# A two-block recurrence and feed-forward kernel on one core: residuals by transposes, expert masks on GpSimd, the last slot in channel chunks, and a new order on every engine

## The chip, the cores and the metric

The kernel runs on one core of a Trainium2 chip. The time is device microseconds (us) from start to end of one execution, the median of several runs. The five engines are TensorE (PE, with its weight loads as PEld), VectorE (DVE), ScalarE (ACT), GpSimd (POOL) and SyncE (SP), which here only issues transfers. Each runs its own list of instructions in the order in which the program wrote them, and waits on semaphores for the others.

## The reference

Four batches ("slots" b = 0 to 3) of x, 256 positions by 256 channels, go through two blocks. The core of it, shortened:

```python
x = x + moe(bi_wkv(x, side, side, w0, u0, cond), A, Bw, Wg)
x = x + ffn(bi_wkv(x, side, side, w1, u1, cond), w1, b1, w2, b2)

def bi_wkv(r, k, v, w, u, t):       # per channel, along the 256 positions
    ek = exp(min(k, 30)); ekv = ek * v
    nf, df = forward scans of a = a * decay + (ekv or ek)
    nb, db = the same scans backward
    euk = exp(min(u + k, 30))
    return sigmoid(r) * (nf + nb - ekv + euk * v) / max(df + db - ek + euk, 1e-8) * (0.8 + 0.2 * tf)

def moe(x, A, Bw, Wg):              # 8 experts of rank 64, the best one per position
    prob = softmax(x @ Wg.T); chosen = argmax(prob)
    return (((x @ A.T) * onehot(chosen)) @ Bw) * 4 * prob[chosen]

def ffn(x, w1, b1, w2, b2):         # 1024 hidden units, weights made -1, 0 or 1
    return gelu(x @ q(w1).T + b1) @ q(w2).T + b2
    # q(w) = sign(w) where |w| >= 0.7 * mean(|w|), else 0
```

## The kernel before, in words

Everything is transposed on chip: channels lie on the 128 partitions (two chunks, c = 0 and 1) and positions along the free dimension. A layer's slot passes through these helpers, whose names and lines the prediction uses:

- `forward` and `backward` (scans, lines 794 and 828, two instructions of 128x256 each) for the numerator (NUM) and the denominator (DEN), on DVE. Between the two `seed` (line 286) rescales the last column. `own_keys` (778, DVE), `own_values` (242), `add_num` (248) and `times_sigmoid` / `times_tanh` (254, 265) are the rest of the numerator, mostly on POOL; `add_den` (835) is the rest of the denominator.
- The reciprocal is `log_den` and `reciprocal` on ACT (529, 534), one Newton step on DVE (`den_times_rec` 840, then `ratio` 857, or `refine_rec` 846 and `product` 863), and `num_times_rec` (405) on POOL.
- The expert block: `gate_logits` (1141), `gate`, `gate_index` and `expert_mask` (870 to 892) on DVE, `transpose_mask`, `expert_in` (1156, fp32, in two halves k), `select_expert` (900, DVE), and `expert_out` (1172, fp32), which accumulates on the residual that `place_residual` (1130) put into its bank. `keep_x1` (599) copies the sum out.
- The feed-forward block: `xin_high` and `xin_low` (306 or 305, and 292) split the input into two fp32r parts; `hidden(b, j)` (1224) multiplies both parts with a quarter of w1, 8 matmuls; `gelus` (611, ACT); `h_high` and `h_low` (305 or 306, and 298) split h; `ffn_out(b, j, n)` (1258) multiplies with a quarter of w2 for half n of the positions, 4 matmuls, onto what `place_output` (1250) put there.
- `keep_warm(n)` and `warm_up(n)` (1041, 1035) are transposes whose results are not used.

Each engine's order is a flat list of such calls at the end of its block (POOL from line 418, ACT from 614, DVE from 909, PE from 1266); nothing else sets the order. A helper that takes an engine as its first argument can be put on DVE, POOL or ACT. The two placings multiply fp32 data with the fp32 identity:

```python
pe.matmul(bank[Y_BANK][:, c * T + n * P:c * T + (n + 1) * P],
          x_nat[:, NT * b + n, c * P:(c + 1) * P], ident[:, :], start=(c == 0 and n == 0), stop=False)
```

The expert mask compares a row of expert numbers with the chosen expert's number and multiplies by its probability. On DVE its three inputs lie in PSUM, which POOL cannot be given here:

```python
dve.tensor_scalar(mask[:, i % (2 * NT)], expert_ps, bank[DVE_BANK][:, IDX_AT + i:IDX_AT + i + 1],
                  bank[DVE_BANK][:, GREC_AT + i:GREC_AT + i + 1], ALU.is_equal, ALU.mult).then_inc(mask_ready, 1)
```

Results leave through two staging buffers: `result` (slots 0 to 2) and `last_result` (two halves of slot 3).

Of the kernel before, what the change touches and what calls it, by code (L numbers as in the profile page):

```python
# [6 lines left out]
ALU = mybir.AluOpType  # L7
# [17 lines left out]
def adaln_ffn_kernel(nc, x, fside, cond, w_l0, u_l0, A, Bw, Wg, w_l1, u_l1, w1, b1, w2, b2, out):  # L25
# [23 lines left out]
    with ExitStack() as ctx:  # L49
# [51 lines left out]
        gsum = sb("gsum", [P, NI])  # L101
        mask = sb("mask", [P, 2 * NT, P])
# [75 lines left out]
        g_bank = [7, 4] * 4 + [6, 7, 4] * 2 + [6, 7]  # L178
# [3 lines left out]

        NEG_AT, IDX_AT, GREC_AT, EXPERT_AT = 4 * ND, 4 * ND + 2, 4 * ND + 2 + NI, P
# [5 lines left out]
        expert_ps = bank[DVE_BANK][:, EXPERT_AT:EXPERT_AT + P]  # L189
# [112 lines left out]

        def copy_on(eng, dst, src):
# [77 lines left out]
        def _(pool):  # L381
# [24 lines left out]

            def factors():
# [15 lines left out]
            seed(pool, 0, 0, DEN)  # L423
            seed(pool, 0, 1, DEN)
            seed(pool, 0, 0, NUM)
            times_values(pool, 1)
            own_values(pool, 0, 0)
            clip_keys(pool, 2)
            add_num(pool, 0, 0)
            times_sigmoid(pool, 0)  # L430
            own_values(pool, 0, 1)
            seed(pool, 0, 1, NUM)
            num_times_rec(0, 0)
            add_num(pool, 0, 1)
            seed(pool, 0, 2, DEN)
            times_values(pool, 2)
            times_sigmoid(pool, 1)
            num_times_rec(0, 1)
            clip_keys(pool, 3)
            own_values(pool, 0, 3)  # L440
            own_values(pool, 0, 2)
            seed(pool, 0, 3, DEN)
            times_values(pool, 3)
            seed(pool, 0, 2, NUM)
            add_num(pool, 0, 2)
            times_sigmoid(pool, 2)
            num_times_rec(0, 2)
            seed(pool, 0, 3, NUM)
            own_values(pool, 1, 0)
            add_one(0)  # L450
            seed(pool, 1, 0, NUM)
            add_num(pool, 0, 3)
            times_sigmoid(pool, 3)
            seed(pool, 1, 0, DEN)
            num_times_rec(0, 3)
            add_num(pool, 1, 0)
            times_tanh(pool, 0)
            add_b2(0)
            num_times_rec(1, 0)
# [3 lines left out]
            add_one(1)  # L463
            xin_low(pool, 0)
            own_values(pool, 1, 2)
            seed(pool, 1, 1, NUM)
            own_values(pool, 1, 3)
# [3 lines left out]
            seed(pool, 1, 2, DEN)  # L471
            add_b2(2)
            xin_low(pool, 1)
            h_low(pool, 0, 1)
            seed(pool, 1, 2, NUM)
            add_one(2)
            h_low(pool, 0, 2)
            add_num(pool, 1, 2)
            h_low(pool, 1, 0)
            h_low(pool, 1, 2)  # L480
            h_low(pool, 1, 3)
            add_one(3)
            h_low(pool, 2, 0)
            add_b2(3)
            h_low(pool, 3, 1)
            h_low(pool, 3, 3)

        @block.scalar
        def _(act):
# [115 lines left out]

            def gelus(b, j):
# [791 lines left out]
```

## Time and profile before

| | us |
|---|---|
| median of 3 runs (103.58 to 103.70) | 103.62 |
| the profiled execution's own time | 102.58 |
| its span, first to last instruction or transfer | 100.8 |
| PE busy in the span | 93.5 |
| DVE busy | 86.7 |
| ACT busy | 80.2 |
| POOL busy | 66.1 |

The profiled execution is 1.8 us longer than its span (start and end of the program) and 1.0 us under the median. "Busy" is the union of an engine's records. Matmul records overlap, since matmuls are pipelined: what one costs is the distance between starts. Transfers fill the first 20 us (inputs, 5.26 MB) and then only the outputs remain.

### The profile page before, as it was taken

What the parts mean: (1) busy time and instruction counts of PE and PEld (TensorE: products, weight loads), DVE (VectorE), ACT (ScalarE), POOL (GpSimd) and SP (SyncE); (2) the same over time, 40 slices, a digit from 0 to 9 for tenths busy, and PEclk for the clock granted to TensorE, in tenths of its full rate; (3) what the DMA queues carried; (4) which work ended last, traced back from release to release, by engine and by line L of the source; (5) the groups of instructions that cost most, each with busy time, mean ns of one, the idle gap of its engine ahead of it and who ended that gap; (6) DMA issues with size and microseconds to landing.
All of it is one profiled execution on the core that took longest, in us unless ns stands there. A gap on an engine that the chain in (4) does not pass through costs nothing. (4 is left out here: it accounts for less than half of the span.)

```text
span 100.8 us, 2134 instructions
## 1 busy us (share of the span) xinstructions
PE 93.5 (93%) x665; PEld 85.0 (84%) x665; DVE 86.7 (86%) x203; ACT 80.2 (80%) x144; POOL 66.1 (66%) x90
## 2 busy tenths in 40 slices
PE   3999779989988999999999999999999999999980
PEld 2688659978878889888888888989999999999970
DVE  3389999999999999999999999999997997883330
ACT  4369999999986679999667499998986899986520
POOL 4058679979984796069868987999980867005310
DMA  1899999700000000000000000000000020200005
GB/s 33 243 292 336 298 228 385 281 3 0 3 0 0 3 0 7 0 0 0 0 3 7 0 0 0 0 0 0 0 7 0 0 104 33 72 7 3 0 0 208
DMA packets 6886, 6.43 MB, mean 64 GB/s; under 512 B 2370, under 2 KB 6492, under 8 KB 6876
## 3 DMA queue, kind: packets, MB, share of 16 engines
q1 hardware_dynamic: 6868, 6.31, 20.2%
q8 instruction: 5, 0.08, 0.3%
q14 instruction: 5, 0.04, 0.1%
q10 hardware_dynamic: 8, 0.00, 0.0%
HBM read 5.26 MB, written 1.05 MB: 63 GB/s over the span
## 5 line engine op out<-in xcount | busy, mean ns | idle before, releaser
L298 POOL TENSOR_TENSOR h_lo<-h,h_hi 128x512 fp32r<-128x512 f32 x9 | 12.3, 1367 | 12.5 <-DVE h_hi L306 7.1
L794 DVE TENSOR_TENSOR_SCAN run<-bank,kv 128x256 f32<-128x256 f32 x32 | 20.1, 674 | 0.2
L1156 PE MATMUL bank<-num,AT 128*128 128x256 f32 x64 | 15.5, 384 | 0.7 <-DVE hm L900 0.5
L1258 PE MATMUL bank<-w2T,h_hi 128*128 128x256 f32 x64 | 15.9, 286 | 0.0
L611 ACT ACTIVATE h<-bank,bT 128x256 f32<-128x256 f32 x32 | 13.1, 478 | 3.2 <-PE bank L1224 2.9
L1224 PE MATMUL bank<-xin_hi,w1T 128*128 128x256 f32 x64 | 15.5, 283 | 0.0
L1258 PE MATMUL bank<-w2T,h_lo 128*128 128x256 f32 x64 | 15.6, 281 | 0.0
L1224 PE MATMUL bank<-xin_lo,w1T 128*128 128x256 f32 x64 | 15.2, 277 | 0.0
L1172 PE MATMUL bank<-hm,BT 128*128 128x256 f32 x64 | 14.6, 381 | 0.0
L1156 PEld LDWEIGHTS bank<-num,AT 128*128 128x128 f32 x64 | 11.6, 190 | 2.2 <-issue 0.9
L1172 PEld LDWEIGHTS bank<-hm,BT 128*128 128x128 f32 x64 | 11.9, 190 | 1.5
L1224 PEld LDWEIGHTS bank<-xin_hi,w1T 128*128 128x128 f32 x64 | 12.0, 188 | 0.6 <-POOL xin_lo L292 0.4
L248 POOL TENSOR_TENSOR num<-num,own 128x512 f32<-128x512 f32 x7 | 8.9, 1278 | 5.2 <-DVE num L828 5.1
L1258 PEld LDWEIGHTS bank<-w2T,h_lo 128*128 128x128 f32 x64 | 12.0, 188 | 0.0
L1258 PEld LDWEIGHTS bank<-w2T,h_hi 128*128 128x128 f32 x64 | 12.0, 188 | 0.0
L1224 PEld LDWEIGHTS bank<-xin_lo,w1T 128*128 128x128 f32 x64 | 12.0, 188 | 0.0
L242 POOL TENSOR_TENSOR own<-own,vs 128x512 f32<-128x512 f32 x8 | 10.2, 1275 | 1.4 <-DVE own L778 1.3
L828 DVE TENSOR_TENSOR_SCAN bank<-bank,run 128x256 f32<-128x256 f32 x16 | 10.2, 681 | 0.0
L828 DVE TENSOR_TENSOR_SCAN num<-bank,run 128x256 f32<-128x256 f32 x16 | 10.1, 671 | 0.0
L405 POOL TENSOR_TENSOR num<-num,run 128x512 f32<-128x512 f32 x5 | 6.4, 1279 | 1.2 <-DVE run L794 0.9
L529 ACT ACTIVATE run<-bank 128x512 f32<-128x512 f32 x8 | 4.8, 605 | 2.9 <-DVE bank L835 2.9
L305 ACT ACTIVATE h_hi<-h 128x512 fp32r<-128x512 f32 x11 | 6.8, 635 | 0.3 <-ACT h L611 0.2
(141 smaller groups left out, 226.1 us busy)
## 6 DMA issues: line engine op xcount, KB each, us to landing
w_nat<-in_L_ffn_w_dram SPq DMA_DIRECT2D x2, 1024.0 KB, 8.5
F_nat<-in_fside_BxSxS_dram SPq DMA_DIRECT2D x4, 256.0 KB, 3.1
x_nat<-in_x_dram SPq DMA_DIRECT2D x4, 256.0 KB, 4.9
out_dram<-outb SPq DMA_DIRECT2D x3, 256.0 KB, 2.1
A_nat<-in_L_ffn_A_dram SPq DMA_DIRECT2D x1, 512.0 KB, 5.6
B_nat<-in_L_ffn_Bw_dram SPq DMA_DIRECT2D x2, 256.0 KB, 6.3
out_dram<-outb SPq DMA_DIRECT2D x2, 128.0 KB, 1.9
wv_rows<-in_L_cond_w_dram SPq DMA_DIRECT2D x2, 1.0 KB
```

Of the source, the lines that this page charges most:

```text
L242: eng.tensor_tensor(own[:, r, :, NUM, :], own[:, r, :, DEN, :], vs[:, b], ALU.mult).then_inc(ownv_ready[r], 1)
L248: eng.tensor_tensor(num_at(l, b), num_at(l, b), own[:, r, :, NUM, :], ALU.add).then_inc(num_ready[r], 1)
L298: eng.tensor_tensor(h_lo[:, b % 2, 2 * j:2 * j + 2], h32[:, b % 2, 2 * j:2 * j + 2], h_hi[:, b % 2, 2 * j:2 * j + 2].bitcast(F32), ALU.sub ...
L305: return eng.activation(dst, src, ACT.Copy)
L405: pool.tensor_tensor(num_at(l, b), num_at(l, b), run[:, r, :, DEN, :], ALU.mult).then_inc(q_ready[r], 1)
L611: act.activation(h32[:, b % 2, f], bank[g_bank[NJ * b + j]][:, (f % 2) * T:(f % 2 + 1) * T], ACT.Gelu, bias=bT[:, f:f + 1], scale=0.5).the ...
L794: dve.tensor_tensor_scan(run[:, r, c, q], decay_ps[:, l, c, b:b + 1].broadcast_to([P, T]), kv[:, b, c, q], 0.0, ALU.mult, ALU.add).then_in ...
L828: dve.tensor_tensor_scan(into[:, c, ::-1], decay_ps[:, l, c, b:b + 1].broadcast_to([P, T]), run[:, r, c, q, ::-1], 0.0, ALU.mult, ALU.add) ...
L1156: mm = pe.matmul(bank[H_BANK + k][:, (m % 2) * T:(m % 2 + 1) * T], AT[:, c, m * P:(m + 1) * P], num_at(0, b)[:, c], start=(c == 0), stop=( ...
L1172: mm = pe.matmul(bank[Y_BANK][:, o * T:(o + 1) * T], BT[:, m, o * P:(o + 1) * P], hm[:, b % 2, m], start=False, stop=(o == NC - 1 and m == ...
L1224: mm = pe.matmul(bank[g_bank[g]][:, (f % 2) * T:(f % 2 + 1) * T], w1T[:, c, f * P:(f + 1) * P], part[:, b % 2, c], start=(c == 0 and part ...
L1258: mm = pe.matmul(o_region(b, n), part[:, b % 2, f, n * P:(n + 1) * P], w2T[:, f], start=False, stop=(f == NF - 1 and part is h_lo and (n = ...
```

## The change

1. `place_residual` and `place_output` pass `is_transpose=True`, on the same data and the same identity.
2. `expert_mask` moves to POOL. The chosen number and the reciprocal of the softmax sum go into small SBUF tiles (`chosen`, `prob`) in place of PSUM columns; DVE keeps the reciprocal as `gate_reciprocal`, and no longer copies the row of expert numbers to PSUM.
3. Slot 3 of layer 1: the denominator's steps, the product and the split into xin parts run per channel chunk (`last_...` helpers), each chunk's denominator in a PSUM bank of its own (2 and 3); `last_hidden(j, c)` issues the four matmuls of one chunk. The last quarter of h is split and multiplied per tile f (`last_gelu`, `last_h_high`, `last_h_low`, `last_ffn_out`). `hidden(3, 3)` uses bank 2 in place of 7.
4. The first `expert_in` half no longer waits for the transposed Bw.
5. All four engines' lists are reordered, and some calls change engine: `clip_keys(1)`, `times_tanh(2)`, `times_tanh(3)`, `add_num(1, 3)`, `h_low(0, 3)`, `h_low(2, 2)` and `seed(1, 3, DEN)` go from DVE to POOL; `own_values(1, 3)`, `h_low(1, 0)`, `h_low(1, 2)`, `h_low(3, 1)`, `h_low(3, 3)` and four `seed` calls from POOL to DVE; `xin_high(2)`, `h_high(2, 1)`, `h_high(3, 3)` and `result(0)` to `result(2)` from ACT to DVE; `xin_high(1)`, `h_high(2, 2)`, `h_high(3, 1)` and `last_result(0)` from DVE to ACT.

The diff, cut to its core:

```diff
-                                  x_nat[:, NT * b + n, c * P:(c + 1) * P], ident[:, :], start=(c == 0 and n == 0), stop=False)
+                                  x_nat[:, NT * b + n, c * P:(c + 1) * P], ident[:, :], start=(c == 0 and n == 0), stop=False, is_transpose=True)
...
-                                  start=(c == 0 and (n == 0 or b == NB - 1)), stop=False)
+                                  start=(c == 0 and (n == 0 or b == NB - 1)), stop=False, is_transpose=True)
...
+            def expert_mask(b):
+                pool.wait_ge(consts_ready, 4 + NE)
+                pool.wait_ge(index_steps, (NT + 1) * (b + 1))
+                pool.wait_ge(grec_ready, b + 1)
+                if b >= 2:
+                    pool.wait_ge(mask_psum, b - 1)
+                for i in range(NT * b, NT * (b + 1)):
+                    pool.tensor_scalar(mask[:, i % (2 * NT)], expert_of[:, :], chosen[:, i:i + 1], prob[:, i:i + 1],
+                                       ALU.is_equal, ALU.mult).then_inc(mask_ready, 1)
...
-                dve.tensor_copy(bank[DVE_BANK][:, IDX_AT + NT * b:IDX_AT + NT * (b + 1)], idx8[:, both, 0]).then_inc(index_steps, 1)
+                dve.tensor_copy(chosen[:, both], idx8[:, both, 0]).then_inc(index_steps, 1)
...
+                dve.reciprocal(prob[:, both], gsum[:, both]).then_inc(grec_ready, 1)
...
-        g_bank = [7, 4] * 4 + [6, 7, 4] * 2 + [6, 7]
+        g_bank = [7, 4] * 4 + [6, 7, 4] * 2 + [6, 2]
...
+            def last_den_times_rec(c):
+                dve.wait_ge(rec_ready[LR], LU + c + 1)
+                den = last_den(c)
+                dve.tensor_tensor(den, den, run[:, LR, c, DEN, :], ALU.mult).then_inc(dr_ready[LR], 1)
...
+            def last_hidden(j, c):
+                g = NJ * LB + j
+                pe.wait_ge(xlo_ready[LB % 2], LB // 2 + 1 + c)
+                if c == 0:
+                    hidden_bank_free(g)
+                for f in (2 * j, 2 * j + 1):
+                    for part in (xin_hi, xin_lo):
+                        mm = pe.matmul(bank[g_bank[g]][:, (f % 2) * T:(f % 2 + 1) * T], w1T[:, c, f * P:(f + 1) * P],
+                                       part[:, LB % 2, c], start=(c == 0 and f == 2 * j and part is xin_hi),
+                                       stop=(c == NC - 1 and f == 2 * j + 1 and part is xin_lo))
+                if c == NC - 1:
+                    mm.then_inc(g_psum, 1)
```

The start of the new DVE list, from `decays()` to the first `gate`:

```python
forward_chunk(0, 0, DEN, 0); forward_chunk(0, 0, DEN, 1); inverse_gains(); seed(dve, 0, 0, DEN)
backward(0, 0, DEN); forward(0, 0, NUM); place_factors(); forward(0, 1, DEN); own_keys(0, 0)
backward(0, 0, NUM); add_den(0, 0); forward(0, 1, NUM); forward(0, 2, DEN); own_keys(0, 1)
den_times_rec(0, 0); own_keys(0, 2); ratio(0, 0); backward(0, 1, NUM); seed(dve, 0, 2, DEN); gate(0)
```

Its part from `gate(3)` to the end of slot 3's input:

```python
gate(3); add_den(1, 1); gate_index(3); gate_reciprocal(3); forward(1, 2, NUM); own_keys(1, 2)
backward(1, 1, NUM); forward(1, 2, DEN); select_expert(3, 0); den_times_rec(1, 1); select_expert(3, 1)
refine_rec(1, 1); seed(dve, 1, 2, NUM); seed(dve, 1, 2, DEN); product(1, 1); backward(1, 2, DEN)
add_den(1, 2); backward(1, 2, NUM); forward(1, 3, NUM); den_times_rec(1, 2); forward(1, 3, DEN)
refine_rec(1, 2); seed(dve, 1, 3, NUM); own_keys(1, 3); product(1, 2); xin_high(dve, 2); h_low(dve, 1, 0)
xin_low(dve, 2); own_values(dve, 1, 3); backward(1, 3, NUM); backward_last_chunk(0)
backward_last_chunk(1); add_last_den(0); add_last_den(1); h_low(dve, 1, 2); h_high(dve, 2, 0)
h_low(dve, 1, 1); result(dve, 0); last_den_times_rec(0); refine_last_rec(0); last_product(0)
last_xin_high(0); last_den_times_rec(1); last_xin_low(0); refine_last_rec(1); h_high(dve, 2, 1)
last_product(1); last_xin_high(1); last_xin_low(1)
```

On PE `warm_up(4)` before the x transposes becomes `warm_up(8)`, `keep_warm(19)` and `(27)` become `(19)`, `(15)` and, behind the first `expert_in` half, `(8)`. `transpose_B(1)` comes behind `gate_logits(0)`, and `expert_out(0)` before the first `transpose_weights`. From slot 3's hidden layer on, the PE list is:

```python
last_hidden(0, 0); ffn_out(1, 3, 0); ffn_out(1, 3, 1); last_hidden(1, 0); last_hidden(0, 1)
last_hidden(2, 0); last_hidden(1, 1); last_hidden(3, 0); place_output(3); last_hidden(2, 1)
ffn_out(3, 0, n); ffn_out(2, 1, n); ffn_out(3, 1, n); last_hidden(3, 1); ffn_out(3, 2, n)
ffn_out(2, 2, n); last_ffn_out(6, n); ffn_out(2, 3, n); last_ffn_out(7, n)      # each for n = 0, 1
```

## Rows read from the trace of the kernel before

**Rows 1.** The page's first part: busy time, share of the span, instructions.

```profile
PE 93.5 (93%) x665; PEld 85.0 (84%) x665; DVE 86.7 (86%) x203; ACT 80.2 (80%) x144; POOL 66.1 (66%) x90
```

**Rows 2.** The chain that ended last, in order: start, us, engine, line.

```profile
61.46 0.89 PE bank L1130 x8
62.35 1.83 PE bank L1224 x16
...
65.20 3.46 PE bank L1172 x16
...
93.07 4.75 PE bank L1258 x40
...
97.84 0.42 DVE outb L306
```

**Rows 3.** Timeline of DVE, 46 to 51 us: start, duration, line, operation.

```profile
46.66 1.26 DVE L828 TENSOR_TENSOR_SCAN num<-bank,run 128x256 f32<-128x256 f32 x2
47.83 1.25 DVE L828 TENSOR_TENSOR_SCAN bank<-bank,run 128x256 f32<-128x256 f32 x2
49.00 0.67 DVE L857 SCALAR_TENSOR_TENSOR num<-bank,num 128x512 f32<-128x512 f32 x1
49.59 0.68 DVE L900 TENSOR_TENSOR hm<-bank,mask_rows 128x512 f32<-128x512 f32 x1
```

**Rows 4.** Stretches: us, then busy PE, PEld, DVE, ACT, POOL, PE clock, DMA.

```profile
15.00:20.00 5.00, 5.00 (x46) 4.91 (x46) 5.00 (x9) 5.00 (x10) 4.92 (x5) 1.00 0.93 344
...
70.00:75.00 5.00, 4.95 (x43) 4.78 (x42) 5.00 (x11) 4.97 (x11) 4.33 (x6) 1.00 0.01 3
```

**Rows 5.** Timeline of PE, 12 to 28 us.

```profile
12.69 0.66 PE L1110 MATMUL bank<-ident,A_nat 128*128 128x128 f32 x4 [0.69 <-DMA A_nat<-in_L_ffn_A_dram]
13.28 0.29 PE L1098 MATMUL bank<-ident,Wg_nat 8*128 8x8 f32 x2
...
18.02 3.11 PE L1041 MATMUL bank<-ident 128*128 128x128 f32 x27
21.39 1.06 PE L1141 MATMUL bank<-WgT,num 128*128 128x8 f32 x8 [0.26 <-DVE num L857]
...
24.88 1.05 PE L1130 MATMUL bank<-ident,x_nat 128*128 128x128 f32 x8
25.77 1.89 PE L1156 MATMUL bank<-num,AT 128*128 128x256 f32 x8
```

**Rows 6.** Timeline of DVE: mask, expert selection and slot 3's last input part.

```profile
25.79 0.16 DVE L886 RECIPROCAL bank<-gsum 128x2 f32<-128x2 f32 x1
...
26.73 0.68 DVE L857 SCALAR_TENSOR_TENSOR num<-bank,num 128x512 f32<-128x512 f32 x1
...
62.65 1.28 DVE L900 TENSOR_TENSOR hm<-bank,mask_rows 128x512 f32<-128x512 f32 x2
63.84 0.69 DVE L846 SCALAR_TENSOR_TENSOR bank<-bank,run 128x512 f32<-128x512 f32 x1
...
86.37 0.69 DVE L292 TENSOR_TENSOR xin_lo<-sig,xin_hi 128x512 fp32r<-128x512 f32 x1
```

**Rows 7.** Groups by line with shapes: busy us, mean ns of one.

```profile
L227 POOL TENSOR_SCALAR kv<-ek_raw 128x512 f32<-128x512 f32 x2 | 1.2, 612 | 0.7 <-ACT ek_raw L509 0.6
...
L231 POOL TENSOR_SCALAR kv<-ek_raw 128x256 f32<-128x256 f32 x2 | 0.8, 400 | 3.2 <-ACT ek_raw L513 3.2
```

**Rows 8.** Timeline of DVE: a small instruction and one with two SBUF inputs.

```profile
23.45 0.17 DVE L907 TENSOR_SCALAR thr<-thr 128x2 f32<-128x2 f32 x1
...
73.91 0.67 DVE L265 TENSOR_TENSOR num<-num,sig 128x512 f32<-128x512 f32 x1
```

**Rows 9.** Timeline of POOL at the same two times.

```profile
22.29 1.27 POOL L236 TENSOR_TENSOR kv<-kv,vs 128x512 f32<-128x512 f32 x1
...
74.09 1.63 POOL L298 TENSOR_TENSOR h_lo<-h,h_hi 128x512 fp32r<-128x512 f32 x1 [0.43 <-ACT h_hi L305]
```

**Rows 10.** The last transfers, as SP issues them.

```profile
97.94 0.96 SPq L376 DMA_DIRECT2D out_dram<-outb  x2
```

More of the change, by code:

```diff
@@ L101, in adaln_ffn_kernel @@
         gsum = sb("gsum", [P, NI])
+        chosen = sb("chosen", [P, NI])
+        prob = sb("prob", [P, NI])
         mask = sb("mask", [P, 2 * NT, P])
@@ L718, in _ @@
             gelus(3, 1)
+            h_high(act, 3, 1)
             gelus(3, 2)
             h_high(act, 3, 2)
-            gelus(3, 3)
-            h_high(act, 3, 3)
-            result(act, 2)
+            last_gelu(6)
+            last_gelu(7)
+            last_result(act, 0)
         @block.vector
@@ L956, in _ @@
             select_expert(1, 0)
+            own_keys(0, 3)
+            gate(2)
+            forward(0, 3, NUM)
+            backward(0, 3, DEN)
+            gate_index(2)
+            gate_reciprocal(2)
             add_den(0, 3)
-            forward(1, 0, NUM)
-            gate(2)
+            backward(1, 0, DEN)
             backward(0, 3, NUM)
-            gate_index(2)
-            forward(1, 0, DEN)
+            add_den(1, 0)
+            own_keys(1, 1)
+            select_expert(2, 1)
+            select_expert(2, 0)
@@ L963, in _ @@
+            forward(1, 1, DEN)
+            den_times_rec(1, 0)
             den_times_rec(0, 3)
-            expert_mask(2)
-            backward(1, 0, NUM)
-            backward(1, 0, DEN)
+            ratio(1, 0)
             ratio(0, 3)
-            select_expert(2, 0)
-            add_den(1, 0)
-            select_expert(2, 1)
-            forward(1, 1, DEN)
+            forward(1, 1, NUM)
+            backward(1, 1, DEN)
             gate(3)
-            den_times_rec(1, 0)
+            add_den(1, 1)
@@ L974, in _ @@
             gate_index(3)
-            ratio(1, 0)
-            own_keys(1, 1)
-            backward(1, 1, DEN)
-            own_keys(1, 3)
-            add_den(1, 1)
+            gate_reciprocal(3)
+            forward(1, 2, NUM)
             own_keys(1, 2)
-            forward(1, 1, NUM)
-            expert_mask(3)
             backward(1, 1, NUM)
+            forward(1, 2, DEN)
+            select_expert(3, 0)
             den_times_rec(1, 1)
-            select_expert(3, 0)
             select_expert(3, 1)
@@ L998, in _ @@
-            times_tanh(dve, 2)
+            refine_rec(1, 2)
             seed(dve, 1, 3, NUM)
-            seed(dve, 1, 3, DEN)
-            refine_rec(1, 2)
+            own_keys(1, 3)
             product(1, 2)
-            h_low(dve, 0, 3)
-            h_low(dve, 1, 1)
-            xin_low(dve, 2)
-            backward(1, 3, DEN)
-            backward(1, 3, NUM)
-            add_den(1, 3)
-            add_num(dve, 1, 3)
-            h_high(dve, 2, 0)
-            times_tanh(dve, 3)
-            den_times_rec(1, 3)
@@ L1013, in _ @@
-            refine_rec(1, 3)
-            product(1, 3)
-            xin_high(dve, 3)
-            xin_low(dve, 3)
+            xin_high(dve, 2)
+            h_low(dve, 1, 0)
+            xin_low(dve, 2)
+            own_values(dve, 1, 3)
+            backward(1, 3, NUM)
+            backward_last_chunk(0)
+            backward_last_chunk(1)
+            add_last_den(0)
+            add_last_den(1)
+            h_low(dve, 1, 2)
+            h_high(dve, 2, 0)
+            h_low(dve, 1, 1)
+            result(dve, 0)
@@ L1329, in _ @@
             hidden(1, 1)
+            place_output(1)
             ffn_out(0, 1, 0)
```

445 lines of the change are left out of this document (257 added, 188 removed).

## The prediction

> **What bounds the kernel now.** I read four views. The page's first part [rows 1] shows PE busy 93% and DVE 86%; neither figure is a verdict, because matmul records overlap. The chain of waits [rows 2] says where the end comes from: from 61.46 us on it runs through PE alone, and from expert_out(3) at 65.20 to the last copy at 97.84 PE never waits. Further back it goes over to DVE, and DVE's timeline [rows 3] shows why: its instructions start one behind the other with no pause. From these starts come my DVE units: a pair of scans 1.17 us (46.66 to 47.83 to 49.00), a 128x512 instruction 0.59 (49.00 to 49.59). So there are two full engines: DVE decides when PE gets its inputs, up to about 64 us, and PE's own work decides the rest. The stretches [rows 4] show the same (all four compute engines full in 15 to 20 us and nearly so in 70 to 75), and a granted PE clock of 1.00 (2.4 GHz) in both.
>
> **The placings.** A placing is 4 fp32 matmuls in 8 records. From its start to the next group's is 0.89 us (24.88 to 25.77) [rows 5]. The same instruction as a transpose is one record: four cost 0.59 us (12.69 to 13.28), and in a long row 27 take from 18.02 to about 21.1, 0.115 each, so four would cost 0.46. The floor is that 0.46 and the ceiling 0.89, no gain at all. I take 0.50, between the two rows for real transposes, so 0.39 saved per placing and 3.1 us over eight, on the engine that is never idle at the end. The rows show no transpose that opens an accumulation; if the mode change itself costs something it is inside the ceiling.
>
> **The first slot.** gate_logits(0) starts at 21.39 [rows 5], released by DVE's ratio(0, 0). The new DVE list puts behind that ratio a backward pair for the denominator (1.17), one for the numerator (1.17) and an add_den (0.59), and clip_keys(1) leaves for POOL (0.34). Before it come own_keys(0, 2), two instructions of 128x256 (0.8), and a seed (0.1). That is -3.27 + 0.9 = -2.4, so gate_logits(0) can start at 19.0. The POOL work behind it also has to fit: own_values, add_num, times_sigmoid and num_times_rec are four instructions of the 1.27 us kind [rows 9], behind own_keys(0, 0) at about 12.1, so 17.4 at best, with DVE needing it at 18.4: hidden by one microsecond. If POOL slips by more, ratio(0, 0) slips with it.
>
> **The masks.** On DVE two masks and their reciprocal take 25.79 to 26.73 [rows 6], 0.94 us, of which about 0.15 (the reciprocal) stays: 0.79 saved per slot, 3.1 over four. On POOL no such instruction is to be seen. One input at 128x256 costs 0.40 and at 128x512 0.61 [rows 7]; by their slope a 128x128 one is 0.3. The ends are 0.2 (a quarter of 0.61 and no fixed cost) and the 1.27 of a two-input 128x512. I take 0.3, because the shape lies next to the 0.40. Two per slot make 0.6, and POOL has room (66% busy [rows 1]). The mask waits for the gate's index and reciprocal, with num_times_rec, times_tanh or seed queued behind it on POOL; by my walk POOL reaches it about when the gate is done or earlier by under 1 us, and what stands behind it waits for a later DVE scan anyway.
>
> **Up to expert_out(3).** Two sums must meet. PE: from gate_logits(0) to expert_out(3) took 65.20 - 21.39 = 43.8 us. Five placings fall in it (-1.95), and keep_warm(8) (+0.9) and transpose_B(1) (+0.56) come into it, so 43.3, and 19.0 + 43.3 = 62.3. DVE: select_expert(3, 1) was over at 63.84 [rows 6]. Removed in front of it are the masks (3.1), the clip (0.34) and own_keys(1, 3) (0.79); added are both forward pairs of slot (1, 2) instead of none (2.34) and seeds (0.15). That gives 63.84 - 1.74 = 62.1. Both sums say that expert_out(3) starts at 62.3, 2.9 us earlier. That is the front of the gain: ratio(0, 0) earlier for PE, masks off DVE, and neither engine alone would give it. It assumes that the gaps in PE's list, which I count at about 3 us from gate_logits(0) on, stay as they are.
>
> **After expert_out(3).** Here the work is the same but for three placings, 1.2 us less. So PE would be done at 97.84 - 2.9 - 1.2 = 93.7, 4.1 us earlier. The cover to check is slot 3. Its last input part ended at 86.37 + 0.69 = 87.06 [rows 6], 0.2 us ahead of PE. In the new list DVE loses before that point masks 3.1, clip 0.34, two times_tanh and an add_num 1.8, h_low(0, 3) 0.6, xin_high(1) 0.35 and some 1.3 of its own waits, 7.5 in all, and gains own_values 0.6, two h_low 1.2, xin_high(2) and h_high(2, 1) 0.7, result(0) 0.6, seeds 0.3 and 0.5 for splitting five instructions into chunks: 3.9. So the second chunk is there at 83.4 and the first some 1.5 earlier, 81.9, while PE reaches last_hidden(0, 0) at about 82.2. In ACT the new list puts slot 3's logarithm, exponential and two table loads before gelus(2, 1), which by the same count ends at 81.3. Three engines thus arrive within a microsecond of each other. With no slack on any, I put 0.5 us down for the join; the chunks are what keeps it so small, since PE may start with the first half.
>
> **The end.** The last copy and its transfer are as before: SP issues two stores from 97.94 [rows 10]. result(2) now runs on DVE some 0.5 us before the last copy on the same engine, and may push it by 0.1, which I leave inside the 0.5.
>
> **Sum.** -2.9 - 1.2 + 0.5 = -3.6 us on the profiled execution, whose time is 102.58 (span 100.8 and 1.8 around it): 99.0. The median of the runs is 1.04 above that execution, so I forecast 103.62 - 3.6 = 100.0.
>
> **Rivals.**
> - *Only the placings pay.* The order is so tight that any slip on POOL or ACT (their work has no measured counterpart in the new order) opens a gap on PE, and the earlier start is waited away. Then the 5 placings from 61.46 on are left, 2.0 us: 101.6. For it speaks that DVE, PE and ACT are all full in 70 to 75 us [rows 4]; against it that two independent sums give the same start.
> - *The order closes gaps too.* Of the 3 us of PE's gaps up to 61 us, one goes as well and the join is free: 103.62 - 5.1 = 98.5.
> - *The transposes save nothing.* Placings stay at 0.89; 3.1 of the gain goes, and 0.5 is left: 103.1. Rows for transposes of loaded data [rows 5] speak against it.
> - *VectorE and GpSimd get in each other's way*, the case in which it becomes slower. POOL's h_low at 74.09 took 1.63 us instead of 1.27, while DVE's times_tanh at 73.91 also read two SBUF tensors [rows 8, 9]: 0.36 lost. The change puts such instructions on DVE while POOL is at work (own_values(1, 3), h_low(1, 0), h_low(1, 2), xin_low(2), xin_high(2), h_high(2, 0), h_high(2, 1)), and makes the four copies into `chosen` and the four reciprocals into `prob` SBUF to SBUF. If each of these 15 waited on DVE for half a POOL instruction, 0.64, DVE would be 9.6 us later in all, of which the sums above cover 4.1 and about 0.5 of slack: 5.0 late, 108.6. It turns slower once the mean wait of the 15 passes 0.3. Against it: the 128x2 instruction at 23.45 is SBUF to SBUF, fell into POOL's 22.29 to 23.56, and took 0.17 with no delay [rows 8, 9]. The Trainium skill (SBUF — State Buffer, Who interferes with whom) says that VectorE and GpSimd share a port pair, locked for a whole instruction by whichever starts first, when VectorE copies within SBUF in a two-port mode or has two SBUF inputs. By that rule the small copies would stall, and the time would be the one of this rival; the trace's small row speaks against it for the small ones, and the 1.63 speaks for it for the large ones.
>
> **Chances.** Forecast 0.48, more than that (98.5) 0.12, only the placings 0.22, transposes save nothing 0.06, port conflict 0.09 and some other wait with no gain 0.03. A measurement here can tell about 0.2% from no change. Faster: 0.48 + 0.12 + 0.22 + 0.05 = 0.87; within 0.2% 0.04; slower 0.09. The range for 8 in 10 takes in the better case partly and the placings alone: 98.7 to 102.4 us, leaving out the two last cases and the ends of the others.
>
> **What would show it.** Placings: L1130 and L1250 with half the records, 0.5 us to the next group. First slot: gate_logits(0) near 19.0. Masks: POOL instructions of 128x128 near 0.3, and DVE free of them. expert_out(3) near 62.3, PE then without pauses, slot 3's first matmuls near 82.5, last copy near 94.2. The forecast is wrong if DVE shows instructions well over their old durations (port conflict), if PE waits for POOL's xin_low or h_low, or if slot 3's reciprocal on ACT comes late.

## The result and the profile after

The changed kernel takes **105.06 us** (median of 4 runs, 104.09 to 105.27) where the kernel before, in the same session, takes 103.60 (4 runs, 103.51 to 103.70). The ratio is 1.0142 with a 95% interval of 1.0086 to 1.0197: slower by 1.4%, where 100.0 us and a range of 98.7 to 102.4 had been forecast. The executions of either kernel differ in the granted TensorE clock, and like must be compared with like. The kernel before ran 43 times beside the experiments below; nine of these were slow ones (more than 1.5% above the fastest) and are left out. Of the other 34, 20 held a mean clock of 0.995 or more (median 102.57 us) and 14 had 0.983 or less (median 103.57). The changed kernel took 104.09 in its one execution at 1.00 and 105.0, 105.13 and 105.27 at 0.983 to 0.984. The change costs 1.5 to 1.6 us at either clock.

The rows below are of the profiled execution of the changed kernel (105.0 us, span 103.2, clock 0.983). First its page, busy time as in [rows 1] and the group of the new masks:

```profile
PE 90.8 (88%) x633; PEld 81.3 (79%) x633; DVE 91.2 (88%) x206; ACT 79.0 (77%) x144; POOL 72.2 (70%) x96
L423 POOL TENSOR_SCALAR mask<-expert_of,chosen,prob 128x128 f32<-128x128 f32 x8 | 6.3, 797 | 2.3 <-DVE prob L974 2.3
```

DVE gave up the masks and is nevertheless busy for 91.2 us instead of 86.7. The last part of the chain of waits, beside [rows 2] (start, us, engine, line):

```profile
86.79 1.28 issue
88.06 0.42 DVE sig L911
...
88.51 0.30 DVE xin_hi L916
...
88.84 0.44 DVE xin_lo L921
...
89.32 2.11 PE bank L1330 x16
91.42 0.44 PE bank L1357 x4
...
98.09 0.96 PE bank L1365 x8
```

Before, the chain ran in PE from 61.46 us on. Now it comes to PE only at 89.32 us; ahead of that it goes through DVE's last input part of slot 3. What stands there as "issue" for 1.28 us is DVE inside one instruction. DVE's timeline shows it (start, duration, line, operation):

```profile
22.61 0.88 DVE L968 CAST chosen<-idx 128x2 f32<-128x2 uint32 x1
...
73.55 1.33 DVE L314 CAST xin_hi<-sig 128x512 fp32r<-128x512 f32 x1
...
75.40 1.09 DVE L292 TENSOR_TENSOR xin_lo<-sig,xin_hi 128x512 fp32r<-128x512 f32 x1
...
80.01 1.70 DVE L298 TENSOR_TENSOR h_lo<-h,h_hi 128x512 fp32r<-128x512 f32 x1
81.63 0.41 DVE L314 CAST h_hi<-h 128x512 fp32r<-128x512 f32 x1
81.97 0.68 DVE L298 TENSOR_TENSOR h_lo<-h,h_hi 128x512 fp32r<-128x512 f32 x1
...
84.54 0.65 DVE L916 CAST xin_hi<-sig 128x256 fp32r<-128x256 f32 x1
...
85.45 0.93 DVE L921 TENSOR_TENSOR xin_lo<-sig,xin_hi 128x256 fp32r<-128x256 f32 x1
...
86.63 1.51 DVE L314 CAST h_hi<-h 128x512 fp32r<-128x512 f32 x1
```

The same form has two durations: h_lo takes 1.70 and then 0.68, the h_hi cast 0.41 and then 1.51. POOL's timeline at these times tells which is which:

```profile
22.18 1.28 POOL L254 TENSOR_TENSOR num<-num,sig 128x512 f32<-128x512 f32 x1
...
79.87 1.29 POOL L265 TENSOR_TENSOR num<-num,sig 128x512 f32<-128x512 f32 x1
...
84.99 1.10 POOL L274 TENSOR_TENSOR x_nat<-x_nat,bT 128x512 f32<-128x512 f32 x1
86.56 1.29 POOL L298 TENSOR_TENSOR h_lo<-h,h_hi 128x512 fp32r<-128x512 f32 x1 [0.47 <-ACT h_hi L313]
```

POOL's times_tanh starts at 79.87 and ends at 81.16; DVE's h_lo, begun at 80.01, ends at 81.71, 0.55 behind it, which is about its own length. POOL's h_lo ends at 87.85, DVE's cast at 88.14, 0.29 behind it. Each of the long DVE instructions is an ordinary one that first waits out the POOL instruction that was already under way. There are seven, and together they lose 0.71 + 0.90 + 0.40 + 1.01 + 0.36 + 0.51 + 1.10 = 5.0 us. The reciprocals into `prob`, which are also SBUF to SBUF, do not wait: this one lies well inside POOL's instruction and takes its usual 0.15.

```profile
33.00 0.15 DVE L974 RECIPROCAL prob<-gsum 128x2 f32<-128x2 f32 x1
...
32.55 1.28 POOL L254 TENSOR_TENSOR num<-num,sig 128x512 f32<-128x512 f32 x1
```

On PE the waits show so:

```profile
76.55 0.39 PE L1317 MATMUL bank<-xin_hi,w1T 128*128 128x256 f32 x1 [1.51 <-DVE xin_lo L292]
...
86.43 0.39 PE L1330 MATMUL bank<-xin_hi,w1T 128*128 128x256 f32 x1 [0.20 <-DVE xin_lo L921]
...
89.32 0.39 PE L1330 MATMUL bank<-xin_hi,w1T 128*128 128x256 f32 x1 [0.77 <-DVE xin_lo L921]
```

### The profile page after: what moved, and what is told of

The parts are those of the page before. It is cut to its first block, busy times and chain, and to the rows that moved or that the text cites. A ratio compares the mean times of both kernels' runs of the same rounds, so it can differ in the third digit from the quotient of the medians.

```text
span 103.2 us, 2087 instructions
## 1 busy us (share of the span) xinstructions
PE 90.8 (88%) x633; PEld 81.3 (79%) x633; DVE 91.2 (88%) x206; ACT 79.0 (77%) x144; POOL 72.2 (70%) x96
## 4 chain that ended last, share of the span: by engine, by line
PE 38%; DVE 25%; ACT 18%; issue 14%; DVEq 1%; POOL 1%; POOLq 0%
PE bank L1267 9%; PE bank L1365 6%; PE bank L1251 5%; DVE bank L862 4%; PE bank L1129 4%; PE bank L1330 3%; DVE run L828 3%; PE bank L1160 3%; DVE num L862 2%; DVE h_lo L298 2%; ACT sig L567 2%; PE bank L1235 2%; DVE bank L874 2%; PE bank L1135 2%; PE bank L1291 1%
## 5 line engine op out<-in xcount | busy, mean ns | idle before, releaser
L1267 PE MATMUL bank<-hm,BT 128*128 128x256 f32 x64 | 16.3, 412 | 0.2 <-issue 0.2
L248 POOL TENSOR_TENSOR num<-num,own 128x512 f32<-128x512 f32 x8 | 10.3, 1286 | 4.7 <-DVE num L862 4.4
L1317 PE MATMUL bank<-xin_hi,w1T 128*128 128x256 f32 x48 | 11.9, 287 | 1.5 <-DVE xin_lo L292 1.5
L1317 PE MATMUL bank<-xin_lo,w1T 128*128 128x256 f32 x48 | 11.5, 279 | 0.0
L1317 PEld LDWEIGHTS bank<-xin_hi,w1T 128*128 128x128 f32 x48 | 9.0, 188 | 1.9 <-DVE xin_lo L292 1.7
L298 POOL TENSOR_TENSOR h_lo<-h,h_hi 128x512 fp32r<-128x512 f32 x7 | 9.3, 1346 | 1.5 <-DVE h_hi L314 1.0
L1317 PEld LDWEIGHTS bank<-xin_lo,w1T 128*128 128x128 f32 x48 | 9.1, 189 | 0.0
L423 POOL TENSOR_SCALAR mask<-expert_of,chosen,prob 128x128 f32<-128x128 f32 x8 | 6.3, 797 | 2.3 <-DVE prob L974 2.3
L298 DVE TENSOR_TENSOR h_lo<-h,h_hi 128x512 fp32r<-128x512 f32 x8 | 6.5, 813 | 1.2 <-ACT h_hi L313 1.1
L812 DVE SCALAR_TENSOR_TENSOR own<-ek_raw,bank 128x256 f32<-128x256 f32 x16 | 6.9, 470 | 0.0
```

The costliest lines, as they stand in the source:

```text
L248: eng.tensor_tensor(num_at(l, b), num_at(l, b), own[:, r, :, NUM, :], ALU.add).then_inc(num_ready[r], 1)
L298: eng.tensor_tensor(h_lo[:, b % 2, 2 * j:2 * j + 2], h32[:, b % 2, 2 * j:2 * j + 2], h_hi[:, b % 2, 2 * j:2 * j + 2].bitcast(F32), ALU.sub ...
L423: pool.tensor_scalar(mask[:, i % (2 * NT)], expert_of[:, :], chosen[:, i:i + 1], prob[:, i:i + 1], ALU.is_equal, ALU.mult).then_inc(mask_r ...
L812: dve.scalar_tensor_tensor(own[:, r, c, DEN], ek_raw[:, b, c], scale_ps[:, l, c, b:b + 1], cap_ps[:, l, c, b:b + 1].broadcast_to([P, T]), ...
L1267: mm = pe.matmul(bank[Y_BANK][:, o * T:(o + 1) * T], BT[:, m, o * P:(o + 1) * P], hm[:, b % 2, m], start=False, stop=(o == NC - 1 and m == ...
L1317: mm = pe.matmul(bank[g_bank[g]][:, (f % 2) * T:(f % 2 + 1) * T], w1T[:, c, f * P:(f + 1) * P], part[:, b % 2, c], start=(c == 0 and part ...
```

## The experiments

All times are medians; the kernel before, measured anew beside each set of runs, took 103.47 to 103.55 us.

**1. The placings alone.** The kernel before, with nothing but the two placings made transposes:

```diff
-    ident[:, :], start=(c == 0 and n == 0), stop=False)
+    ident[:, :], start=(c == 0 and n == 0), stop=False, is_transpose=True)
...
-    start=(c == 0 and (n == 0 or b == NB - 1)), stop=False)
+    start=(c == 0 and (n == 0 or b == NB - 1)), stop=False, is_transpose=True)
```

> The kernel before with one edit: both placings as transposes, nothing else of the change. Theory A (VectorE's slot 3 holds the end): in the kernel before, slot 3's last input part was ready at 87.06 us and TensorE reached it at 87.24, and seven of the eight placings lie ahead of that point, so TensorE would only wait for VectorE instead. Only 0.2 us come back at once, and at most the 1.3 us that VectorE waited for ScalarE at 77.8 and 83.7: 0.3 to 1.5 us faster than before, 102.1 to 103.3. Theory B (the prediction's: TensorE's own work from 61 us on is the end, so each placing pays): 2.0 to 3.1 us faster, 100.5 to 101.6. Both expect half the records and 0.35 to 0.5 us from a placing to the next group.

It took 102.76 us (10 runs), ratio 0.9928 (0.9873 to 0.9983): a gain of 0.8 us (0.2 to 1.3) from an edit that takes 8 x 0.45 = 3.6 us of work from PE. PE's timeline of this kernel, with the last placing and the matmuls behind it:

```profile
86.65 0.60 PE L1250 MATMUL bank<-ident,x_nat 128*128 128x128 f32 x4
87.77 0.38 PE L1224 MATMUL bank<-xin_hi,w1T 128*128 128x256 f32 x1 [0.52 <-DVE xin_lo L292]
```

PE waits for slot 3's input, which ends at 87.02 + 0.69 = 87.71 on DVE. Already in the kernel before, that input had only 0.2 us in hand. So PE's work by itself was not what the end could be shortened by: the interval leaves out the 2.0 us and more that it would have given.

The same trace shows, on DVE and POOL, the instruction on which the prediction's argument against the port conflict rests:

```profile
23.40 1.21 DVE L907 TENSOR_SCALAR thr<-thr 128x2 f32<-128x2 f32 x1
...
23.31 1.28 POOL L254 TENSOR_TENSOR num<-num,sig 128x512 f32<-128x512 f32 x1
```

In the kernel before it took 0.17 [rows 8]. Here POOL began 0.09 us ahead of it, and it ends at 24.61, 0.02 behind POOL: 1.04 us of waiting for two columns. Everything behind it on DVE is later by about as much (select_expert(3, 0) starts at 63.62 instead of 62.65), so this one execution, of 103.12 us, does not tell how long PE would have waited without it. Of the executions of this kernel at a clock of 0.995 or more, four took 101.87 to 102.19 us and three 103.07 to 103.41; whether this wait is what parts them is not shown, since only one was profiled.

**2. The changed kernel with the placings as matmuls.**

```diff
-    ident[:, :], start=(c == 0 and n == 0), stop=False, is_transpose=True)
+    ident[:, :], start=(c == 0 and n == 0), stop=False)
...
-    start=(c == 0 and (n == 0 or b == NB - 1)), stop=False, is_transpose=True)
+    start=(c == 0 and (n == 0 or b == NB - 1)), stop=False)
```

> The changed kernel with fp32 matmuls for the placings again. Theory A (VectorE is late in slot 3, TensorE has slack ahead of it): only the placing behind slot 3's first matmuls is on the path, 0.4 us, and a part of the others: 0.4 to 1.2 us slower than the changed kernel's 105.1. Theory B (TensorE bound): 3.1 us slower. If the transposes themselves brought the low granted clock at 29 to 34 us, the clock would be 1.00 here and the time 1 us better for it.

105.2 us, 1.0184 (1.003 to 1.0338). Against the changed kernel at like clock that is 0.1 to 0.7 more (104.2 and 104.68 to 104.09; 105.71 to 105.0 to 105.3), 0.1 in the medians: less than the 0.4 to 1.2 expected, and nothing like the 3 us and more of PE's time that the edit puts back. In two of its four runs the clock fell as well (0.984), so the transposes are not needed for the dip.

**3. The clock held.** Nine transposes into an unused bank ahead of place_residual(0):

```diff
+            def hold_warm(n):
+                pe.wait_ge(BT_ready, 2)
+                for _ in range(n):
+                    pe.transpose(bank[Y_BANK][:, 0:P], ident[:, :], ident[:, :])
...
             weight_totals()
+            hold_warm(9)
             place_residual(0)
```

> The changed kernel with nine unused transposes ahead of the first placing, where TensorE stood idle for 0.98 us before gate_logits(1). Theory of the clock (too little TensorE work in 24 to 29 us lets the granted clock fall): clock 1.00 in every slice, expert_out(0) back from 5.12 to 3.5 us, and the time at the 104.1 of the one run with a clock of 1.00, that is 0.5 to 1.0 us less than 105.1. Rival (the fall has another cause, or VectorE is the bound there): the clock or the time stays.

104.66 us, 1.0155 (1.005 to 1.0261); the clock stayed at 0.996 or more in all four. The stretches of the changed kernel (us, busy PE, PEld, DVE, ACT, POOL, then the clock):

```profile
25.00:30.00 5.00, 3.65 (x22) 2.83 (x21) 4.97 (x11) 3.46 (x4) 3.57 (x5) 0.91 0.01 2
30.00:35.00 5.00, 5.00 (x25) 4.14 (x24) 4.93 (x18) 4.23 (x7) 4.34 (x6) 0.75 0.01 2
```

and of this one:

```profile
25.00:30.00 5.00, 4.82 (x35) 4.41 (x34) 4.97 (x13) 3.51 (x4) 3.14 (x4) 1.00 0.00 2
30.00:35.00 5.00, 5.00 (x36) 4.32 (x34) 4.93 (x17) 4.90 (x9) 4.76 (x6) 1.00 0.01 2
```

Without the nine, PE is busy 3.65 of 5 us, then runs part of the next 5 us at 1.2 instead of 2.4 GHz. expert_out(0) takes 3.69 us here and 5.28 there, and expert_out(3) starts at 63.61 instead of 64.48. Not all of these 0.87 us are the clock's: gate_logits(0), which lies ahead of the nine transposes, already starts at 19.14 instead of 19.56. The other 0.45 are the clock's, as far as one execution of each can tell. The median is 0.4 lower, just under the 0.5 to 1.0 expected, and the two kernels' executions overlap (104.04 to 105.18, and 104.09 to 105.27), so a gain in the whole time is not shown by this experiment alone.

**4. result(2) on ACT.**

```diff
             last_gelu(7)
+            result(act, 2)
             last_result(act, 0)
...
-            result(dve, 2)
             last_result(dve, 1)
```

> The changed kernel with result(2) on ScalarE, ahead of last_result(0), so that VectorE has only the very last copy to make. Theory (the new end costs a microsecond: 4.0 us from the last matmul to the end of the span against 3.0 before, because result(2)'s copy and store stand in front of the last ones): 0.4 to 1.0 us faster than 105.1, the last copy about 0.6 us earlier. Rival (the stores land one behind the other anyway): within 0.2 us.

104.99 us, 1.0179 (1.0089 to 1.0269): no change, as the rival had it. The first of the last stores goes out at 99.69 instead of 99.79, because what it copies is ready no earlier: ffn_out(2, 3) still stands near the end of PE's list.

**5. The POOL instructions shortened.** times_tanh(3), h_low(2, 0), h_low(2, 2) and add_b2(3) handle 32 of 256 positions; the rest of their work is left out.

```diff
-            eng.tensor_tensor(num_at(1, b), num_at(1, b), sig[:, b], ALU.mult).then_inc(nsig_ready[b], 1)
+            W = 32 if b == 3 else T
+            eng.tensor_tensor(num_at(1, b)[:, :, 0:W], num_at(1, b)[:, :, 0:W], sig[:, b, :, 0:W], ALU.mult).then_inc(nsig_ready[b], 1)
...
+            W = 32 if eng is nc.gpsimd and (b, j) in ((2, 0), (2, 2)) else T
```

> The changed kernel with four late GpSimd instructions (times_tanh(3), h_low(2, 0), h_low(2, 2), add_b2(3)) cut to 32 of the 256 positions of each chunk; the rest of their output is left out. Theory A (the lock: a VectorE instruction that reads two SBUF tensors or copies within SBUF waits for the GpSimd instruction under way): the h_low at 80.0, the two xin parts at 84.5 and 85.4 and the h_high at 86.6 go back from 1.70, 0.65, 0.93 and 1.51 us to 0.69, 0.29, 0.43 and 0.42, slot 3's last input part comes 2.5 to 3 us earlier, and the time falls by 1.0 to 2.5 us below the changed kernel's. Rival (those durations have another cause, such as the fp32r conversion or ScalarE's traffic): the durations stay and the time changes by less than 0.5.

102.89 us (10 runs), 0.9959 (0.9911 to 1.0006): 2.2 us less than the changed kernel, although none of the shortened instructions is on DVE. DVE's timeline:

```profile
81.34 0.73 DVE L301 TENSOR_TENSOR h_lo<-h,h_hi 128x512 fp32r<-128x512 f32 x1
82.00 0.41 DVE L317 CAST h_hi<-h 128x512 fp32r<-128x512 f32 x1
...
85.77 0.29 DVE L919 CAST xin_hi<-sig 128x256 fp32r<-128x256 f32 x1
...
86.31 0.41 DVE L924 TENSOR_TENSOR xin_lo<-sig,xin_hi 128x256 fp32r<-128x256 f32 x1
...
86.98 0.41 DVE L317 CAST h_hi<-h 128x512 fp32r<-128x512 f32 x1
```

The four late instructions of 1.70, 0.65, 0.93 and 1.51 have become 0.73, 0.29, 0.41 and 0.41, in the same order and with the same operands. The two that were at 73 to 76 us (here at 74.88 and 76.73), whose POOL neighbours keep their length, still take 1.33 and 1.09. This settles the cause of the long instructions. (This profiled execution had a clock of 0.967, so its starts are not compared.)

**6. The small cast through PSUM.** In place of the one cast into `chosen`, one into PSUM and a copy out of it:

```diff
-    dve.tensor_copy(chosen[:, both], idx8[:, both, 0]).then_inc(index_steps, 1)
+    dve.tensor_copy(bank[DVE_BANK][:, at:at + NT], idx8[:, both, 0]).then_inc(chosen_psum, 1)
+    dve.wait_ge(chosen_psum, b + 1)
+    dve.tensor_copy(chosen[:, both], bank[DVE_BANK][:, at:at + NT]).then_inc(index_steps, 1)
```

> The changed kernel with the chosen expert's number written to PSUM first and copied from there to SBUF, so that no copy reads and writes SBUF. Theory A (the lock takes small copies too): the 0.88 us copy at 22.6 is gone, two copies of 0.16 in its place and the next add_den starts 0.6 us earlier relative to gate_index. Rival: the 0.88 us has another cause and stays in one of the two. Time within 0.6 us of the changed kernel.

One execution: 104.17 us at a clock of 1.00, which is the changed kernel's 104.09 at that clock. On DVE:

```profile
22.27 0.16 DVE L970 CAST bank<-idx 128x2 f32<-128x2 uint32 x1
22.46 0.16 DVE L972 COPY chosen<-bank 128x2 f32<-128x2 f32 x1
```

Both run inside POOL's instruction of 21.82 to 23.10 and neither waits. So the 0.88 came from reading and writing SBUF in one instruction, and the mend is worth 0.5 us at that place: the next add starts 0.27 us after the cast instead of 0.79. In the time of the whole kernel this one execution shows nothing of it.

**7. The masks back on DVE,** with the index, the expert numbers and the reciprocal in PSUM as before:

```diff
-                    pool.tensor_scalar(mask[:, i % (2 * NT)], expert_of[:, :], chosen[:, i:i + 1], prob[:, i:i + 1],
-                                       ALU.is_equal, ALU.mult).then_inc(mask_ready, 1)
...
+                    dve.tensor_scalar(mask[:, i % (2 * NT)], bank[DVE_BANK][:, EXPERT_AT:EXPERT_AT + P], bank[DVE_BANK][:, IDX_AT + i:IDX_AT + i + 1],
+                                      bank[DVE_BANK][:, GREC_AT + i:GREC_AT + i + 1], ALU.is_equal, ALU.mult).then_inc(mask_ready, 1)
```

> The changed kernel with the four pairs of masks back on VectorE, from PSUM, in the place of gate_reciprocal. VectorE gets 4 x 0.79 = 3.1 us more, less 0.7 for the copy that no longer waits. Theory A (VectorE is the bound up to slot 3): 2.0 to 3.0 us slower than the changed kernel, 107 to 108. Rival (the mask on GpSimd costs as much there, at 0.80 us each instead of the 0.3 forecast, as it saved): within 1 us of the changed kernel.

107.75 us, 1.0442 (1.0331 to 1.0552): 2.7 us more than the changed kernel. Two of the four executions had a clock of 0.968, lower than any of the changed kernel's; the two at 0.982 and 0.984 took 107.18 and 107.27, which is 2.1 more at like clock. The masks are four pairs of 0.75 us on DVE, 3.0 in all, and in the profiled execution (clock 0.968) expert_out(3) starts at 68.09 instead of 64.48. Moving them was the part that paid, in spite of 0.80 each on POOL.

**8. The tail alone.** result(2) on ACT as in 4, and on PE:

```diff
-            last_ffn_out(6, 0)
-            last_ffn_out(6, 1)
             ffn_out(2, 3, 0)
             ffn_out(2, 3, 1)
+            last_ffn_out(6, 0)
+            last_ffn_out(6, 1)
```

> The changed kernel with only its end mended: result(2) on ScalarE, and ffn_out(2, 3) ahead of last_ffn_out(6), so that slot 2's store starts 0.47 us earlier. The stores are issued one behind the other, 0.42 us each, behind result(2). Theory (the last 4.0 us hang on result(2), and e4 changed nothing because its matmuls stood where they were): 0.4 to 0.6 us faster than the changed kernel at like clock, and 3.4 to 3.6 us from the last matmul's start to the end of the span. Rival (the last copy sets the end): no change, as in e4.

104.8 us, 1.0154 (1.0096 to 1.0212), all four at a clock of about 0.983, so 0.3 less than the changed kernel at its like, a little under the 0.4 to 0.6 expected. Of the span it is more: 102.5 to 102.9 against 103.2 to 103.4 at that clock. SP's stores, of the changed kernel:

```profile
99.79 0.37 SPq L380 DMA_DIRECT2D out_dram<-outb  x1
100.21 0.95 SPq L384 DMA_DIRECT2D out_dram<-outb  x2
```

and of this one:

```profile
99.18 0.37 SPq L380 DMA_DIRECT2D out_dram<-outb  x1
99.64 0.91 SPq L384 DMA_DIRECT2D out_dram<-outb  x2
```

The kernel before had this too:

```profile
97.52 0.37 SPq L372 DMA_DIRECT2D out_dram<-outb  x1
```

The stores leave one behind the other: the next one followed 0.42 us later in the kernel before [rows 10] and in the changed one, and 0.46 later here. But before, the store of result(2) left as the last matmul began (97.53). In the changed kernel it leaves 0.56 us behind the start of the last matmul (99.23), when the last two are nearly ready, and they queue behind it.

**9. Slot 3's moves alone.** On the changed kernel, what met a POOL instruction goes to ACT or away from POOL:

```diff
 pool:   add_one(3)
+            add_b2(3)
             add_num(pool, 1, 3)
-            times_tanh(pool, 3)
             h_low(pool, 2, 0)
             h_low(pool, 1, 3)
-            add_b2(3)
-            h_low(pool, 2, 2)
 act:    gelus(1, 2)
+            xin_high(act, 2)
...
             gelus(2, 3)
+            h_high(act, 2, 1)
 dve:    product(1, 2)
-            xin_high(dve, 2)
...
             add_last_den(1)
+            times_tanh(dve, 3)
             h_low(dve, 1, 2)
...
-            h_high(dve, 2, 1)
...
             h_low(dve, 2, 1)
+            h_low(dve, 2, 2)
```

> The changed kernel with only the moves around slot 3: xin_high(2) and h_high(2, 1) back on ScalarE, times_tanh(3) and h_low(2, 2) on VectorE, add_b2(3) earlier on GpSimd. Nothing is left out. Theory A (the lock): these remove the waits of 0.9, 1.0, 0.5 and 1.1 us, slot 3's last input part comes near 86.5 instead of 89.3, and the time falls by 1.5 to 2.5 us below the changed kernel's 105.1. Rival: the moves only shift work between full engines, less than 0.5.

102.66 us (10 runs), 0.9956 (0.991 to 1.0001): 2.4 us less than the changed kernel, although what came to DVE (two instructions of 0.68) is by its own duration more than what left it (two of 0.41). Its timeline:

```profile
73.26 1.71 DVE L298 TENSOR_TENSOR h_lo<-h,h_hi 128x512 fp32r<-128x512 f32 x1
...
75.49 1.09 DVE L242 TENSOR_TENSOR own<-own,vs 128x512 f32<-128x512 f32 x1
...
80.10 0.68 DVE L298 TENSOR_TENSOR h_lo<-h,h_hi 128x512 fp32r<-128x512 f32 x1
...
83.62 0.65 DVE L916 CAST xin_hi<-sig 128x256 fp32r<-128x256 f32 x1
...
86.09 0.43 DVE L921 TENSOR_TENSOR xin_lo<-sig,xin_hi 128x256 fp32r<-128x256 f32 x1
```

The last part is done at 86.52 instead of 89.27. The wait at 73 us was not removed but handed on: with the cast gone, the h_lo behind it meets POOL's pair.

**10. All of it together:** hold_warm(9), `chosen` through PSUM, the tail of 8 and the moves of 9.

> The changed kernel with all mends together: nine transposes ahead of the first placing, the chosen number by way of PSUM, result(2) on ScalarE and ffn_out(2, 3) ahead of last_ffn_out(6), xin_high(2) and h_high(2, 1) back on ScalarE, times_tanh(3) and h_low(2, 2) on VectorE, add_b2(3) on GpSimd while it is idle at 76. If lock, clock and end are the causes: 0.6 + 0.5 (clock) + 0.5 (end) + 2 (slot 3) off 105.1, so 101.3 to 102.3, faster than both kernels. If the order of the engines itself is what costs: above 103.5.

101.94 us (4 runs), 0.9884 (0.9793 to 0.9975): within the range, and faster than both kernels. The same kernel once more, beside the last one:

> The mended kernel e8 once more, unchanged, beside its successor: 101.6 to 102.3 us, and about 1.5% faster than the kernel before.

101.84 us (6 runs), 0.9866 (0.9825 to 0.9907), 1.3% less than the kernel before.

**11. The order at 73 us changed too,** so that a scan, which reads PSUM, stands where POOL's pair of h_lo is under way:

```diff
             product(1, 2)
+            backward(1, 3, NUM)
             h_low(dve, 1, 0)
             xin_low(dve, 2)
-            own_values(dve, 1, 3)
-            backward(1, 3, NUM)
...
             add_last_den(1)
+            own_values(dve, 1, 3)
+            add_num(dve, 1, 3)
             times_tanh(dve, 3)
```

> The mended kernel e8 with a new order of VectorE between product(1, 2) and slot 3's reciprocal, and add_num(1, 3) on VectorE: the numerator's backward pair stands where h_low(1, 0) waited for 1.0 us, and own_values(1, 3) comes when GpSimd is idle. Theory A: the 1.71 and 1.09 us instructions at 73.3 and 75.5 fall to 0.69, the last input part comes 0.8 us earlier and TensorE's waits of 0.7 and 0.3 shrink: 0.3 to 1.0 us faster than e8, 101.0 to 101.6. Rival (TensorE is the bound again in e8): within 0.2 us of it.

101.63 us (6 runs), ratio 0.9837 (0.9793 to 0.9882) to the kernel before: the fastest version measured, though only 0.2 us under the one of 10 that ran beside it, and the intervals overlap. So the gain of 0.3 to 1.0 us did not come, although the waits went. DVE has no lengthened instruction left between 72 and 87 us:

```profile
72.95 1.26 DVE L863 TENSOR_TENSOR_SCAN num<-bank,run 128x256 f32<-128x256 f32 x2
74.13 0.66 DVE L299 TENSOR_TENSOR h_lo<-h,h_hi 128x512 fp32r<-128x512 f32 x1
...
77.14 0.68 DVE L243 TENSOR_TENSOR own<-own,vs 128x512 f32<-128x512 f32 x1
...
85.40 0.42 DVE L922 TENSOR_TENSOR xin_lo<-sig,xin_hi 128x256 fp32r<-128x256 f32 x1
```

PE, busy 89.7 of 99.8 us, still waits 0.9 us for xin_lo(2) and 0.6 twice for the expert selection.

## Why the prediction was wrong, step by step

The forecast for the profiled execution was 99.0; it took 105.0. Three stretches hold the 6.0 us: up to expert_out(3) +2.2, from there to the last matmul +3.6, the end +0.7, less the 0.5 that had been allowed for the join.

**The bound: half right.** "PE's own work decides the rest" was read from a chain without a wait in it [rows 2]. Experiment 1 shows what such a chain leaves out: a DVE part that is ready only 0.2 us ahead of it is the next bound. The prediction named that 0.2 us and still credited PE's savings in full, since it took the new order to bring DVE forward as well. "Only the placings pay", worked out at 101.6, fails for the same reason: alone they gave 0.8 us (0.2 to 1.3), not 2.0.

**The placings: right.** Forecast 0.50 for each; the chain has 0.44, in 4 records for 8.

**The first slot: nearly right.** gate_logits(0) started at 19.56, forecast 19.0.

**The masks: size wrong, step right.** 0.80 each, not 0.3; the nearest row (one input, 128x256, 0.40) has no factor read from memory for each partition; whether that is the reason was not tested. It cost little, as POOL had room, and experiment 7 puts the step at 2.7 us, 2.1 at like clock, where the forecast took 3.1 off DVE.

**Up to expert_out(3): the start was 64.48, not 62.3.** 0.6 is from gate_logits(0). From there on it took 44.9 us where the forecast had 43.3. Of these 1.6 the clock has 0.45: with the clock held, experiment 3 takes 44.5. The forecast took 1.00 from its rows [rows 4] and did not ask what the new order does to it. PE's list now has 0.98 us of waiting ahead of gate_logits(1), with short transposes in place of matmuls before it, and behind that the clock is 0.75 in 30 to 35 us. Experiment 6, at a clock of 1.00 and with the cast mended, takes 44.55 (19.22 to 63.77); the 1.2 us that are left against 43.3 were not taken apart.

**Slot 3's cover: this is the step that failed.** "The second chunk is there at 83.4" summed undisturbed durations. It was there at 89.27. DVE's select_expert(3, 1) ended 1.8 us late (63.87 against 62.1), and six instructions behind it lost 4.3 us to POOL: 6.1 together, where the measured lateness is 5.9. Experiments 5 and 9 confirm it from both sides: shorten POOL's instructions and DVE's shrink; move DVE's and the kernel is 2.4 us faster.

**The rival that came true was named and given 0.09.** It put 15 x 0.64 on DVE and 108.6 on the kernel. Of its 15, five waited, 4.1 us in all; two more that it had not named, the split of slot 3's first chunk, lost 0.9. Seven waits of 0.71 in the mean: the price of one was about right and the count was half. None of the four reciprocals into `prob` took over 0.17, one of them well inside a POOL instruction, and two of the casts met an idle POOL. What was held against the rival, the row at 23.45 with 0.17 inside POOL's 22.29 to 23.56 [rows 8, 9], could not tell: it ends at 23.62, after POOL's end by less than its own length, and so may itself have waited for that end. In experiment 1 the same instruction begins 0.09 us after POOL's and takes 1.21. In the changed kernel one of the same size, the cast into `chosen`, begins 0.43 us after POOL's and takes 0.88. The Trainium skill (SBUF — State Buffer, Who interferes with whom) says that whichever engine starts first keeps the shared port pair for its whole instruction and that copies and casts within SBUF may claim it, as do two SBUF inputs. By that rule the runs come out as they did, with both kinds waiting; the trace agrees, by the seven instructions above and by experiment 6, where the same cast takes 0.16 once one side of it lies in PSUM. The prediction had let one small row outweigh it.

**The end: 0.7 short.** From the last matmul's start to the end of the span it was 3.27 us before and 3.97 after, 3.35 in experiment 8. The forecast had 0.1 for result(2) on DVE; the cost was in its store on SP's queue, and experiment 4 shows that moving its copy to another engine changes nothing.

**The offset of 1.04.** The forecast added the distance of the median from the profiled execution as if it were fixed. It is no constant: the kernel before has executions of two kinds, 102.57 us in the median at a clock of 0.995 or more and 103.57 at 0.983 or less, 1.0 apart, and the profiled one was of the first kind. The clock is not all of it, since four executions at 0.999 or more took 103.44 to 103.62. The forecast's 100.0 was thus a sum for one kind of execution with the offset of the other.

What stays open: what exactly makes the clock dip after 28 us and why it does so in some executions and not in others; why some executions at full clock take 1 us more; and the rest of the distance to 62.3 at expert_out(3).

## What to carry to other kernels

Before an instruction with two SBUF inputs, or a copy, a cast or a TENSOR_SCALAR from SBUF to SBUF, is put on VectorE, ask which GpSimd instruction will be under way at that time, and price it at that one's remaining length, not at its own duration. A row that shows no wait counts as evidence only if it ended well inside the other engine's instruction. And where two engines end within a few tenths of a microsecond of each other, work taken from one is worth only that gap: take away from the later one first.

## What the runs showed of the hardware

- A VectorE cast of 128x2, SBUF to SBUF, took 0.88 us when it began 0.43 us into a GpSimd instruction, and 0.16 with one side in PSUM. A TENSOR_SCALAR of 128x2 took 1.21 us when it began 0.09 us into one (experiment 1). How long they took was set by what was left of GpSimd's instruction, not by their own size. A RECIPROCAL of 128x2, SBUF to SBUF, took 0.15 us well inside a GpSimd instruction of 1.28.
- It works the other way round too: GpSimd's add_one at 75.05 took 0.91 us, where 0.61 is usual for its shape [rows 7], as VectorE's h_lo of 74.80 was under way; the h_lo of 1.63 us in the kernel before [rows 9] is of the same kind.
- GpSimd's compare and multiply with two factors per partition takes 0.80 us at 128x128, more than VectorE's 0.41.
- With nine fp32 transposes where TensorE had waited about 1 us, the mean clock was 0.994 or more in 20 of 20 executions (experiments 3, 10 and 11); without them the changed kernel and its variants of experiments 4 and 8 held it in one of 12, that of experiment 2 in two of four, that of experiment 6 in its only one, and that of experiment 9 reached 0.993 in two of 10.
- Stores issued by SP leave 0.42 to 0.46 us apart in the rows shown, so a third store issued just ahead of the last two holds them up by as much.
